# Wave attention: the value products of four heads in one call, two split heads of four, and the second half of every score on VectorE

## The chip, the cores and the metric

The kernel runs on one core of a Trainium2 chip. The metric is the device time of one execution in microseconds (us). The core has five engines with instruction streams of their own, in order and coupled by semaphores: TensorE (PE; its weight loads are listed as PEld), VectorE (DVE), ScalarE (ACT), GpSimd (POOL) and SyncE (SP), which here issues the DMAs.

## The reference, cut to what matters

Four blocks follow one another on x of 8 x 512 x 128: wave attention, a mixture of experts, an attention with distance terms, and the experts again, each on the layer-normed x and added to it. The change is in wave attention alone, which for 16 heads of 8 columns is:

```python
sim = jnp.einsum('bhid,bhjd->bhij', q, k) / sqrt(hd) / temp
scores = 0
for fi, freq in enumerate([31.0, 37.0, 41.0, 43.0, 47.0]):
    scores = scores + alpha[h, fi] * jnp.sin(TWO_PI * sim / freq + phi[h, fi])
w = sigmoid(scores); w = w / (w.sum(-1) + 1e-10)
out = jnp.einsum('bhij,bhjd->bhid', w, v)
```

So each of the 128 (batch, head) pairs has a 512 x 512 matrix, and each element of it takes five sines, five products with a head's factor, and a sigmoid.

## The kernel before

The heads are taken in NG = 32 groups of HG = 4; a head's 512 x 512 scores lie on 128 partitions as 2048 columns (four blocks kt of 512). Two groups are unrolled into `pair`, which a loop repeats. Head n = 4g + h passes through the engines as follows.

- **Scores.** TensorE makes them in two halves of 1024 columns (`make_scores`, L717, bf16) into psS, which holds one half at a time. Each half is copied to `s` as a fixed-point angle: the first half always by ScalarE (L792), the second by VectorE (L893) for heads in EVAC_HEADS and by ScalarE for the others. This runs two heads ahead of the sums.
- **Angles.** VectorE's `make_angles` turns `s` into the angles of frequencies 1, 2, 4 and 3, in that order (L880), and shifts frequency 4 (L917): five instructions, one head ahead. The angles of frequencies 1 to 3 are written into slots of the ring `score` (eight slots, one per head of two groups) that are free; for heads 2 and 3 some of these slots hold weights of the group before, and VectorE waits for `valued`. Before head 2 it is the last angle, frequency 3, that does. The angles of frequencies 0 to 3 are moved to `wave` by DMAs of 1 MB (L641, the queue SPq).
- **Sines.** ScalarE does five sines of 2048 columns in place (L827).
- **Sums.** TensorE adds frequencies 0 to 2 into psA (four PSUM banks, one copy) as products with diagonal matrices that GpSimd makes (L758). Frequencies 3 and 4 are added by VectorE in halves of 1024 columns (`add_sines`, L927). For a head in SPLIT_HEADS TensorE does frequency 2 for the first half alone, and VectorE adds the second half of it too, as its first instruction (`third`): five adds, without that four. The first add of frequency 3 for a half reads psA, the later ones read `score`. TensorE waits for `added` of the head before, half by half, before it writes psA again.
- **Weights.** ScalarE's `weigh` makes tanh(score / 2) in place (L802), for head n - 2 at the end of head n. The half that turns it into a sigmoid is applied with the column sums of V: L726 sums them into psV, `halve_values` (L923) halves them on VectorE after head 2.
- **Products with the values.** `values` (L734) multiplies the weights of group g - 1 with V, nine columns a head; head h takes rows 32h to 32h + 8 of psO, so a call of two heads goes to two column strips of the array, kt by kt, in turn. Heads 0 and 1 are done behind head 0 of group g, with the sums of L726 ahead of them, heads 2 and 3 behind head 2. `outputs` (L813) copies psO at the end of head 3, and a DMA stores it.

VectorE's order in head h is: angles of the next head, the copy of the second half of head h + 2's scores (if it is VectorE's), the adds of head h. TensorE's order in head h is: first scores of head h + 2, frequency 0, second scores, frequencies 1 and 2, then `values` for h = 0 and 2. The order is written out by hand. A credit (C_WEIGHED and the like) shifts each semaphore's count so that the first heads need no special case. Nothing else in the kernel is touched.

Of the kernel before, what the change touches and what calls it, by code (L numbers as in the profile page):

```python
# [18 lines left out]
H, HD = 16, 8  # L19
QT = L // P  # L20
NT = B * QT
HG = 4
NG = B * H // HG
GPB = H // HG
VW = HD + 1
# [8 lines left out]
MAX_POS = 256  # L34
FAR = 120.0
CARRIED = 4
SPLIT_HEADS = (0, 1, 2, 3)
EVAC_HEADS = (0, 2)
NEAR = 6.0


# [491 lines left out]
def wave_attention(nc, sb, ps, sem, a, V, ident, dram, params, bound):  # L533
# [13 lines left out]
    SR, AR = 2, 2 * HG  # L547
# [4 lines left out]
    CUTS = tuple(range(CARRIED, NF))  # L552
    NCUT = len(CUTS)
    C_SPS, C_SREADY, C_TURNED, C_CUT, C_SINE, C_USED, C_SUMMED = 2 * 2 * HG, 2, 2 * HG * (NF - 1), 2 * HG * NCUT, NF, 2 * PE_F, 4
    C_FIRST, C_VALUED, C_HALF, C_WEIGHED = 2, 4, 1, 2
    C_ADDED, C_DIAG, C_TAKEN, C_STORED = 2 * HG * ADDS, 2 * HG, 2, 16
    with ExitStack() as c:
        qp = sb(c, "qp", [NR, 2, HG, L], BF16)
# [16 lines left out]
        Vg = sb(c, "Vg", [P, 2, QT, HG, P // HG])  # L575
# [6 lines left out]
        psV = ps(c, "psV", [P, 1])  # L582
# [6 lines left out]
        valued = sem(c, "valued")  # L589
# [6 lines left out]
        v_ready = sem(c, "v_ready")  # L596
# [3 lines left out]
        weighed = sem(c, "weighed")  # L600
        out_taken = sem(c, "out_taken")
# [3 lines left out]
        v_summed = sem(c, "v_summed")  # L605
        half_ready = sem(c, "half_v_ready")
# [97 lines left out]
        @block.tensor  # L704
        def _(pe):
            for credit, n in ((s_ps, C_SPS), (s_ready, C_SREADY), (turned, C_TURNED), (first_ready, C_FIRST), (valued, C_VALUED), (cut, C_CUT), (sine, C_SINE),
                              (used, C_USED), (summed, C_SUMMED), (added, C_ADDED), (diag_ready, C_DIAG),
                              (out_taken, C_TAKEN), (half_ready, C_HALF),
                              (weighed, C_WEIGHED),
                              (out_stored, C_STORED)):  # L710
                pe.sem_inc(credit, n)

            def make_scores(n, u, h, half):
                pe.wait_ge(s_ready, n * 2 + half + C_SREADY)
                for k in range(2):
                    kt = half * 2 + k
                    mm = pe.matmul(psS[:, k, :], kp[:, u, h, kt * P:(kt + 1) * P], qp[:, u, h, :],  # L717
                                   start=True, stop=True)
                mm.then_inc(s_ps, 1)

            def values(g, slot, heads):
                if heads[0] == 0:
                    pe.wait_ge(v_ready, g + 1)
                    pe.wait_ge(half_ready, g + C_HALF)
                    for kt in range(QT):
                        mm = pe.matmul(psV[:], Vg[:, slot ^ 1, kt, :, :].rearrange("p h d -> p (h d)"),  # L726
                                       Vg[:, slot ^ 1, kt, 0, HD:VW], start=(kt == 0), stop=(kt == QT - 1))
                    mm.then_inc(v_summed, 1)
                    pe.wait_ge(out_taken, g + C_TAKEN)
                pe.wait_ge(weighed, g * HG + heads[-1] + 1)  # L730
                for kt in range(QT):
                    for h in heads:
                        row = h * (P // HG)
                        mm = pe.matmul(psO[row:row + VW, :],  # L734
                                       Vg[:, slot ^ 1, kt, h, 0:VW],
                                       score[:, slot * HG + h, kt * L:(kt + 1) * L],
                                       start=(kt == 0), stop=(kt == QT - 1), skip_group_check=True)
                mm.then_inc(valued, 1)

            def pair(gg, last):  # L740
                for u in range(2):
                    g = gg * 2 + u
                    for h in range(HG):
                        n = g * HG + h
                        more = not (last and u == 1 and h >= HG - 2)
                        nu, nh = (u, h + 2) if h < HG - 2 else (1 - u, h + 2 - HG)
                        if more:
                            if nh == 0:
                                pe.wait_ge(qk_loaded[nu], (gg + 1 + u) * 32)
                            make_scores(n + 2, nu, nh, 0)  # L750
                        pe.wait_ge(diag_ready, n + 1 + C_DIAG)
                        for f in range(PE_F):
                            pe.wait_ge(sine, n * NF + f + 1 + C_SINE)
                            for kt in range(2 if f == PE_F - 1 and h in SPLIT_HEADS else QT):
                                if f == 0 and kt % 2 == 0:

                                    pe.wait_ge(added, n * ADDS - ADDS + kt // 2 + 1 + C_ADDED)
                                mm = pe.matmul(psA[:, kt, :], diag[:, h % 2, f, :],  # L758
                                               wave[:, h % 2, f, kt * L:(kt + 1) * L],
                                               start=(f == 0), stop=(f == PE_F - 1 or (h in SPLIT_HEADS and f == PE_F - 2 and kt >= 2)),  # L760
                                               skip_group_check=True)
                                if f == PE_F - 1 and (kt % 2 == 1 or h in SPLIT_HEADS):
                                    mm.then_inc(summed, 1)
                            if f < PE_F - 1:
                                mm.then_inc(used, 1)
                            if more and f == 0:
                                make_scores(n + 2, nu, nh, 1)
                        if h in (0, 2):
                            values(g, 1 - u, (h, h + 1))

            pe.wait_ge(qk_loaded[0], 32)
            for h in range(2):
                for half in range(2):
                    make_scores(h, 0, h, half)
            with pe.Fori(0, NG // 2 - 1) as gg:
                pair(gg, False)
            pair(NG // 2 - 1, True)
            for h in (0, 2):
                values(NG, 1, (h, h + 1))

        @block.scalar
        def _(act):
# [13 lines left out]
            def weigh(m, at, general):  # L796
                act.wait_ge(added, (m + 1) * ADDS + C_ADDED)
                if general:
                    act.activation(score[:, at, :], score[:, at, :], ACT.Sigmoid).then_inc(weighed, 1)
                else:  # L800

                    act.activation(score[:, at, :], score[:, at, :], ACT.Tanh, scale=0.5).then_inc(weighed, 1)  # L802
# [13 lines left out]
            def pair(gg, last, general):  # L816
                for u in range(2):
                    g = gg * 2 + u
                    for h in range(HG):
                        n = g * HG + h  # L820
                        more = not (last and u == 1 and h >= HG - 2)
                        for f in range(NF):
                            if f < CARRIED:
                                act.wait_ge(carried[f][h % 2], (g * (HG // 2) + h // 2 + 1) * 16)
                            else:
                                act.wait_ge(cut, n * NCUT + CUTS.index(f) + 1 + C_CUT)
                            act.activation(wave[:, h % 2, f, :], angle[:, h % 2, f, :], ACT.Sin,  # L827
                                           scale=float(TWO_PI / 2.0 ** 32)).then_inc(sine, 1)
                            if f in (2, NF - 1) and more:
                                tu, th, tg = (u, h + 2, g) if h < HG - 2 else (1 - u, h + 2 - HG, g + 1)  # L830
                                if f == 2 or th not in EVAC_HEADS:
                                    take_scores(n + 2, tu, th, tg, f // 4, general)
                        weigh(n - 2, (u * HG + h - 2) % AR, general)
                        if h == HG - 1:
                            outputs(g, 1 - u, general)

            def all_heads(general):
                for h in range(2):
                    take_scores(h, 0, h, 0, 0, general)
                    if h not in EVAC_HEADS:  # L840
                        take_scores(h, 0, h, 0, 1, general)
                act.wait_ge(cleared, 2)
                with act.Fori(0, NG // 2 - 1) as gg:
                    pair(gg, False, general)
                pair(NG // 2 - 1, True, general)
                for h in (HG - 2, HG - 1):
                    weigh((NG - 1) * HG + h, HG + h, general)
                outputs(NG, 1, general)

            act.activation(og[:, 0:1], params[:, 0, 0, 0:1], ACT.Silu)  # L850
# [1276 lines left out]
```

## Time and profile before

| | |
|---|---|
| median of 3 runs (lowest to highest) | 3736.54 us (3734.22 to 3737.48) |
| the profiled execution: time, span | 3738.18 us, 3736.4 us |
| PE, DVE, ACT, POOL busy, share of the span | 84%, 81%, 71%, 26% |
| mean granted clock of TensorE | 0.937 of 2.4 GHz |
| the wave attention stage | about 105 to 1770 us of the span |

The span is that of the core's instructions. Busy shares count an engine as busy when an instruction of it runs; the wait before an instruction is shown with the one that released it. An f32 matmul of TensorE stands in the trace as two records, a bf16 one as one.

### The profile page before, as it was taken

The numbers are of one execution on the slowest core, as the hardware profiler recorded it, in microseconds if no ns is written. First come the engines' busy times: TensorE is split into PE (matmuls) and PEld (weight loads), VectorE is DVE, ScalarE is ACT, GpSimd is POOL, SyncE is SP. The second block draws the span as 40 slices with busy tenths as digits, with TensorE's granted clock in tenths as the row PEclk, the third lists the DMA queues.
The fourth block names the chain that finished last, engine by engine and source line by source line (L and its number), as shares of the span: only waits on it lengthen the run. The fifth ranks groups of instructions, "written<-read, shape, count | busy, mean of one in ns | idle before, by whom it ended". The sixth has DMA issues, their size and how long they took to land. (4 is left out here: it accounts for less than half of the span.)

```text
span 3736.4 us, 70767 instructions
## 1 busy us (share of the span) xinstructions
PE 3127.3 (84%) x26844; PEld 1990.0 (53%) x26844; DVE 3041.0 (81%) x4269; ACT 2656.2 (71%) x2265; POOL 981.3 (26%) x984
## 2 busy tenths in 40 slices
PE   3799999999999999998479715998998998998990
PEld 2233333333333333333358714888887887886890
DVE  8899999999999999997476545878878788786662
ACT  3899999999999999998134214776776776774430
POOL 2111111111111111110005344335245344330436
PEclk9899999999999999999679857999999999997995
DMA  5888899888999888996322227123113122112122
GB/s 163 300 332 343 335 340 346 334 337 337 345 342 340 333 343 337 341 342 253 115 74 60 55 75 183 24 32 51 28 28 51 28 36 42 28 19 74 44 61 68
DMA packets 311331, 683.36 MB, mean 183 GB/s; under 512 B 155296, under 2 KB 228608, under 8 KB 310560
## 3 DMA queue, kind: packets, MB, share of 16 engines
q1 hardware_dynamic: 302368, 661.87, 51.2%
q0 software_dynamic: 8704, 17.84, 2.0%
q8 instruction: 186, 3.05, 0.4%
q14 instruction: 73, 0.60, 0.1%
HBM read 90.73 MB, written 52.10 MB: 38 GB/s over the span
## 5 line engine op out<-in xcount | busy, mean ns | idle before, releaser
L758 PE MATMUL psA<-wave,diag 128*128 128x512 f32 x2560 | 1169.7, 604 | 81.5 <-DVE score L927 66.0
L827 ACT ACTIVATE wave<-wave 128x2048 f32<-128x2048 int32 x640 | 1186.8, 1908 | 44.8 <-DMA wave<-score 38.2
L758 PEld LDWEIGHTS psA<-wave,diag 128*128 128x128 f32 x2560 | 466.6, 190 | 687.7 <-issue 532.3
L880 DVE TENSOR_SCALAR score<-s,par 128x2048 int32<-128x2048 int32 x384 | 480.4, 1278 | 5.9 <-DMA wave<-score 5.8
L690 POOL TENSOR_TENSOR diag<-ident,par 128x128 f32<-128x128 f32 x384 | 143.0, 401 | 1268.7 <-PE psA L758 1268.2
L1850 POOL COPY kb<-ks 48x1024 bf16<-48x1024 bf16 x160 | 321.3, 2008 | 567.1 <-PE psR L1910 380.5
L927 DVE SCALAR_TENSOR_TENSOR score<-wave,par,score 128x1024 f32<-128x1024 f32 x384 | 469.6, 1277 | 0.0
L927 DVE SCALAR_TENSOR_TENSOR score<-wave,par,psA 128x1024 f32<-128x1024 f32 x256 | 315.6, 1274 | 46.7 <-PE psA L758 46.6
L2000 ACT ACTIVATE W<-psR 128x1024 f32<-128x1024 f32 x256 | 249.4, 1023 | 132.5 <-PE psR L1935 132.5
L1991 ACT COPY r<-psR 128x1024 f32<-128x1024 f32 x256 | 248.7, 1020 | 105.0 <-PE psR L1910 104.9
L2037 DVE TENSOR_REDUCE mx<-S 128x8 f32<-128x1024 f32 x256 | 305.4, 1214 | 2.2
L2030 DVE TENSOR_TENSOR S<-psR,S 128x1024 f32<-128x1024 f32 x192 | 234.5, 1221 | 57.0 <-PE psR L1926 56.7
L1935 PE MATMUL psR<-ident,S 128*128 128x128 f32 x2048 | 254.2, 277 | 27.9 <-DVE S L2045 27.9
L802 ACT ACTIVATE score<-score 128x2048 f32<-128x2048 f32 x130 | 247.9, 1907 | 3.5 <-DVE score L927 3.5
L1935 PEld LDWEIGHTS psR<-ident,S 128*128 128x128 f32 x2048 | 226.9, 142 | 40.2 <-DVE S L2030 11.8
L1991 ACT COPY S<-psR 128x1024 f32<-128x1024 f32 x192 | 185.6, 1022 | 82.9 <-PE psR L1910 82.9
L2045 DVE TENSOR_SCALAR S<-S,m 128x512 f32<-128x512 f32 x512 | 242.1, 541 | 0.6
L734 PE MATMUL psO<-score,Vg 128*9 128x512 f32 x1056 | 239.8, 596 | 3.0 <-ACT score L802 3.0
L792 ACT ACTIVATE s<-psS,par 128x1024 int32<-128x1024 f32 x192 | 212.1, 1105 | 11.6 <-PE psS L717 11.5
L1291 POOL DMA_INDIRECT f_xsS<-xn,f_token x144 | 139.5, 968 | 260.1 <-DVE f_token L1420 154.3
L1503 ACT ACTIVATE f_hT<-f_h 128x512 f32<-128x512 f32 x144 | 90.8, 631 | 163.3 <-DVE f_h L1457 163.2
L1926 PE MATMUL psR<-ident,r 128*128 128x128 f32 x1536 | 204.0, 277 | 0.0
(271 smaller groups left out, 4717.3 us busy)
## 6 DMA issues: line engine op xcount, KB each, us to landing
wave<-score SPq DMA_DIRECT2D x384, 1023.9 KB, 6.4
wave<-s SPq DMA_DIRECT2D x128, 1023.9 KB, 4.8
ks<-kb_parts SPq DMA_DIRECT2D x56, 384.0 KB, 6.1
qs<-qb_parts SPq DMA_DIRECT2D x32, 384.0 KB, 6.3
ys<-f_ys SPq DMA_DIRECT2D x36, 256.0 KB, 2.5
wave_out<-og SPq DMA_DIRECT2D x33, 256.0 KB, 7.2
o<-wave_out SPq DMA_DIRECT2D x8, 1024.0 KB, 5.3
qp<-qa_parts SPq DMA_DIRECT2D x32, 192.0 KB, 7.1
```

The lines of the kernel that those rows point to most:

```text
L734: mm = pe.matmul(psO[row:row + VW, :], Vg[:, slot ^ 1, kt, h, 0:VW], score[:, slot * HG + h, kt * L:(kt + 1) * L], start=(kt == 0), stop=( ...
L758: mm = pe.matmul(psA[:, kt, :], diag[:, h % 2, f, :], wave[:, h % 2, f, kt * L:(kt + 1) * L], start=(f == 0), stop=(f == PE_F - 1 or (h in ...
L802: act.activation(score[:, at, :], score[:, at, :], ACT.Tanh, scale=0.5).then_inc(weighed, 1)
L827: act.activation(wave[:, h % 2, f, :], angle[:, h % 2, f, :], ACT.Sin, scale=float(TWO_PI / 2.0 ** 32)).then_inc(sine, 1)
L880: dve.tensor_scalar(out, src, scalar, par[:, u, row, h * NF + f:h * NF + f + 1], ALU.mult, ALU.add).then_inc(done, 1)
L927: return dve.scalar_tensor_tensor(out=score[:, u * HG + h, cols], in0=wave[:, h % 2, f, cols], scalar=par[:, u, 1, h * NF + f:h * NF + f + ...
L1850: pool.tensor_copy(dst[rows, pairs, odd, :], src[rows, :, :].rearrange("r h (n two) -> r n h two", two=2)[:, pairs, :, odd]).then_inc(read ...
L1935: mm = pe.matmul(slot[:, i, kt * P:(kt + 1) * P], S[:, 2 * j + i, kt * P:(kt + 1) * P], ident[:], start=(kt == 0), stop=True, is_transpose ...
L1991: act.copy(dst[:, :, k * CP:(k + 1) * CP], psR[:, n % RING, :, :].rearrange("p a (n h) -> p h (a n)", h=BH)).then_inc(act_took, 1)
L2000: act.activation(W[:, pair % RING_W, :, :].rearrange("p a n -> p (a n)"), psR[:, n % RING, :, :].rearrange("p a n -> p (a n)"), ACT.Exp, s ...
L2037: dve.tensor_reduce(mx[:, hs, kt], S[:, hs, kt * P:(kt + 1) * P], AX.X, ALU.max).then_inc(maxed, 1)
L2045: dve.tensor_scalar(S[:, h, :], S[:, h, :], m[:, h:h + 1], None, ALU.subtract).then_inc(shifted, 1)
```

## The change

SPLIT_HEADS becomes (0, 2): for heads 1 and 3 TensorE sums frequency 2 whole, and VectorE has four adds. EVAC_HEADS becomes (0, 1, 2, 3): VectorE copies the second half of every head's scores. `values` handles all four heads in one call, kt by kt with the four strips in turn, and stands in head 1 between frequency 0 (with the second scores) and frequency 1; it waits for the weights of all four heads of the group before, and `valued` rises by 2 at once. `weigh` handles head n - 1, so that these weights are there in time, and its credit rises to 3.

```diff
-SPLIT_HEADS = (0, 1, 2, 3)
-EVAC_HEADS = (0, 2)
+SPLIT_HEADS = (0, 2)
+EVAC_HEADS = (0, 1, 2, 3)
...
-    C_FIRST, C_VALUED, C_HALF, C_WEIGHED = 2, 4, 1, 2
+    C_FIRST, C_VALUED, C_HALF, C_WEIGHED = 2, 4, 1, 3
...
-            def values(g, slot, heads):
-                if heads[0] == 0:
-                    pe.wait_ge(v_ready, g + 1)
-                    pe.wait_ge(half_ready, g + C_HALF)
-                    for kt in range(QT):
-                        mm = pe.matmul(psV[:], Vg[:, slot ^ 1, kt, :, :].rearrange("p h d -> p (h d)"),
-                                       Vg[:, slot ^ 1, kt, 0, HD:VW], start=(kt == 0), stop=(kt == QT - 1))
-                    mm.then_inc(v_summed, 1)
-                    pe.wait_ge(out_taken, g + C_TAKEN)
-                pe.wait_ge(weighed, g * HG + heads[-1] + 1)
+            def values(g, slot):
+                pe.wait_ge(v_ready, g + 1)
+                pe.wait_ge(half_ready, g + C_HALF)
                 for kt in range(QT):
-                    for h in heads:
+                    mm = pe.matmul(psV[:], Vg[:, slot ^ 1, kt, :, :].rearrange("p h d -> p (h d)"),
+                                   Vg[:, slot ^ 1, kt, 0, HD:VW], start=(kt == 0), stop=(kt == QT - 1))
+                mm.then_inc(v_summed, 1)
+                pe.wait_ge(out_taken, g + C_TAKEN)
+                pe.wait_ge(weighed, g * HG + HG)
+                for kt in range(QT):
+                    for h in range(HG):
                         row = h * (P // HG)
                         mm = pe.matmul(psO[row:row + VW, :],
                                        Vg[:, slot ^ 1, kt, h, 0:VW],
                                        score[:, slot * HG + h, kt * L:(kt + 1) * L],
                                        start=(kt == 0), stop=(kt == QT - 1), skip_group_check=True)
-                mm.then_inc(valued, 1)
+                mm.then_inc(valued, 2)
...
                             if more and f == 0:
                                 make_scores(n + 2, nu, nh, 1)
-                        if h in (0, 2):
-                            values(g, 1 - u, (h, h + 1))
+                            if f == 0 and h == 1:
+                                values(g, 1 - u)
...
-            for h in (0, 2):
-                values(NG, 1, (h, h + 1))
+            values(NG, 1)
...
-                        weigh(n - 2, (u * HG + h - 2) % AR, general)
+                        weigh(n - 1, (u * HG + h - 1) % AR, general)
...
-                for h in (HG - 2, HG - 1):
-                    weigh((NG - 1) * HG + h, HG + h, general)
+                weigh(NG * HG - 1, AR - 1, general)
```

## Rows read from the trace of the kernel before

**Rows 1.** Busy time of each engine in the wave stage; columns in its first line

```profile
core 0: us, PE busy (x) PEld busy (x) DVE busy (x) ACT busy (x) POOL busy (x), PEclk, DMA share, GB/s
...
170.00:1680.00 1510.00, 1420.44 (x4003) 525.43 (x4002) 1472.89 (x1263) 1469.91 (x910) 221.53 (x410) 1.00 0.90 339
```

**Rows 2.** Waits of VectorE and ScalarE, 170 to 1680 us: total, times, longest

```profile
DVE score L927 <- PE psA L758: 37.0, 45, 1.5
...
ACT wave L827 <- DMA wave<-score: 33.3, 65, 1.2
```

**Rows 3.** The halving of the value sums: first of 33, and group 19

```profile
L923 DVE TENSOR_SCALAR half_v<-psV x33: 144/148/153, 159.1 to 1763.5; 128x1 f32<-128x1 f32 x33
...
1136.50 0.15 DVE L923 TENSOR_SCALAR half_v<-psV 128x1 f32<-128x1 f32 x1
```

**Rows 4.** Time line of VectorE, head 0 into head 1: start, us, operation

```profile
1000.54 1.27 DVE L893 TENSOR_SCALAR s<-psS,par 128x1024 int32<-128x1024 f32 x1
1001.74 2.46 DVE L927 SCALAR_TENSOR_TENSOR score<-wave,par,psA 128x1024 f32<-128x1024 f32 x2
1004.12 3.67 DVE L927 SCALAR_TENSOR_TENSOR score<-wave,par,score 128x1024 f32<-128x1024 f32 x3
...
1012.49 1.21 DVE L917 TENSOR_SCALAR wave<-wave 128x2048 int32<-128x2048 int32 x1
1014.61 2.47 DVE L927 SCALAR_TENSOR_TENSOR score<-wave,par,psA 128x1024 f32<-128x1024 f32 x2 [0.91 <-PE psA L758]
```

**Rows 5.** Time line of TensorE's matmuls, heads 0 to 2 of the same group

```profile
1000.90 0.95 PE L726 MATMUL psV<-Vg 128*128 128x1 f32 x8
1001.78 3.61 PE L734 MATMUL psO<-score,Vg 128*9 128x512 f32 x16
1005.32 0.60 PE L717 MATMUL psS<-qp,kp 48*128 48x512 bf16 x2
...
1010.02 5.42 PE L758 MATMUL psA<-wave,diag 128*128 128x512 f32 x12
1015.37 0.60 PE L717 MATMUL psS<-qp,kp 48*128 48x512 bf16 x2
1017.14 3.70 PE L758 MATMUL psA<-wave,diag 128*128 128x512 f32 x8 [1.17 <-DVE score L927]
1020.77 0.60 PE L717 MATMUL psS<-qp,kp 48*128 48x512 bf16 x2
1021.30 5.42 PE L758 MATMUL psA<-wave,diag 128*128 128x512 f32 x12
```

**Rows 6.** Time line of ScalarE: the copy of the first scores in head 1

```profile
1006.38 1.10 ACT L792 ACTIVATE s<-psS,par 128x1024 int32<-128x1024 f32 x1
```

**Rows 7.** TensorE's groups in the second attention, 2340 to 3400 us

```profile
L1935 PE MATMUL psR<-ident,S 128*128 128x128 f32 x2048 | 254.2, 277 | 27.9 <-DVE S L2045 27.9
...
L1951 PE MATMUL psDO<-W,Vb 128*9 128x128 f32 x4096 | 135.8, 273 | 0.0
```

**Rows 8.** Time lines of TensorE behind idle time (in brackets); two windows as in rows 1

```profile
399.56 5.39 PE L758 MATMUL psA<-wave,diag 128*128 128x512 f32 x8 [1.73 <-ACT wave L827]
...
862.62 3.70 PE L758 MATMUL psA<-wave,diag 128*128 128x512 f32 x8 [1.65 <-ACT wave L827]
...
1765.61 5.30 PE L734 MATMUL psO<-score,Vg 128*9 128x512 f32 x16 [2.98 <-ACT score L802]
...
2309.06 1.04 PE L1910 MATMUL psR<-kb,T 112*128 112x64 bf16 x16 [3.40 <-POOL kb L1850]
...
2312.25 0.63 PE L1910 MATMUL psR<-kb,T 112*128 112x64 bf16 x16
...
2322.07 0.89 PE L1923 MATMUL psR<-ks,qs 112*128 112x128 bf16 x8 [2.00 <-ACT W L1991]
...
3363.88 1.94 PE L1935 MATMUL psR<-ident,S 128*128 128x128 f32 x16 [2.21 <-DVE S L2045]
...
3367.45 1.91 PE L1935 MATMUL psR<-ident,S 128*128 128x128 f32 x16
...
400.50:404.50 4.00, 4.00 (x7) 1.54 (x5) 4.00 (x4) 4.00 (x4) 0.00 (x0) 0.57 0.69 262
...
2322.50:2326.00 3.50, 3.50 (x38) 3.44 (x36) 1.22 (x1) 0.44 (x1) 3.01 (x2) 0.55 0.00 0
```

## The prediction

> **What bounds the kernel now.** I read the slices of the page first: the stage of wave attention fills the first half of the span, and the rest is untouched by the change. Over 1,510 us of that stage VectorE is busy for 1,472.9, ScalarE for 1,469.9, TensorE for 1,420.4, at a granted clock of 1.00 (2.4 GHz) [rows 1]. With three engines so full, busy shares decide nothing, so the waits came next: VectorE waits 37.0 us in the stage, and only for TensorE's sums in psA; ScalarE waits 33.3 us for angles carried by DMA [rows 2]. Then the period: the halving of the value sums starts at 159.1 for group 0 and at 1136.50 for group 19, so a group takes 977.4 / 19 = 51.44 us [rows 3]. The 37.0 us are 1.26 per group (1,510 / 51.44 = 29.4 groups); VectorE's own work is the other 50.18. VectorE is in order and nearly full, so the period changes by what its instructions and its waits change.
>
> The time lines show where its waits arise. psA has one copy. TensorE may start head n's first frequency only when VectorE's first add of frequency 3 (the first `added` of head n-1) has read it, and VectorE may start head n's adds only when TensorE has summed again. I call that add's start s. VectorE's pace is 1.19 us an instruction [rows 4]. In [rows 4] the two-instruction row at 1014.61 holds the split add and that add, so s = 1015.80; TensorE starts at 1017.14, s + 1.34 [rows 5]. Its pieces, start to start [rows 5]: frequency 0, 3.63 us (1017.14 to 1020.77); a pair of score matmuls 0.53 (to 1021.30); frequency 1 and half of frequency 2, 5.35 (1010.02 to 1015.37); the sums of values 0.88 and the products of two heads 3.54 (1000.90, 1001.78, 1005.32). Now those 3.54 stand right behind heads 0 and 2, where TensorE would otherwise wait for VectorE's add.
>
> **The change part by part.**
>
> *Split heads (0, 2).* Two VectorE adds go: -2 x 1.19 = -2.38 us a group. TensorE gets two more f32 products in heads 1 and 3 each: a product is 3.44 / 4 = 0.86 (16 records of a 128x512 product at two records each; eight last 3.63 with their tail), so +3.44 a group.
>
> *Second halves of all scores on VectorE.* +2 x 1.20 = +2.40 us a group there, which cancels the above; ScalarE loses two copies of some 1.10 each [rows 6], -2.2 a group. ScalarE's relief is worth its waits at most, and it is not what VectorE waits for. I cost it at nothing.
>
> *`weigh` one head earlier.* The same four per group. It waits for the adds of head n-1; these end 4 x 1.19 = 4.8 us after s, and ScalarE still has the sines of the next head to do. Nothing.
>
> *Four heads at once.* The eight calls for a pair occupy 16 records in 3.54 us; two heads share the array. The new order interleaves four column strips. The nearest row is the second attention, which already does it with 128 columns: 4,096 records in 135.8 us, 33 ns each, where full-width records take 254.2 / 2048 = 124 ns [rows 7]. That is 3.7 to one, so all four heads should take 3.54 once, saving 3.54 per group, against the +3.44. The other bound is pairs only: 7.08. I take 3.54.
>
> *Its new place.* This is the term that matters. The call now stands inside head 1, between frequency 0 and frequency 1, so it is on the path from the first add of head 0 to the first add of head 1, and the idle time behind heads 0 and 2 that covered it is given up. From s of head 0, TensorE needs 1.34 + 3.63 + 0.53 + 0.88 + 3.54, then frequency 1 and, unsplit, kt 0 and 1 of frequency 2: 12 records, 5.42 with their tail, and 0.03 until VectorE starts: s + 15.37. VectorE has that add and three more, five instructions of angles and a copy, ten in all: s + 11.95. It waits 3.42 us. (Within this time `valued` also holds the fourth angle; that wait lies inside the same 3.42, because the sums come last. Queued behind it are the cut and the copy, and the DMA of angle 3 of head 2 starts about 1.7 us later, with over 5 us before its sine is needed.) The second add needs kt 2 and 3, another 1.72, where VectorE is ready after 1.19: +0.53. Together **3.95 us per group, in head 1**.
>
> Head 3, also unsplit: TensorE is ready at s + 1.34 + 3.63 + 0.53 + 5.45 = s + 10.95, VectorE at s + 12.0, and the second add leaves 0.5. No wait, slack 0.5. Heads 0 and 2: TensorE needs 10 records and no values, 1.34 + 3.63 + 0.53 + 4.6 = 10.1 after the add before, VectorE comes at 11.9 or later. The scores' second half in head 1 waits for ScalarE's copy, which in [rows 6] ends at 1007.48, or s + 4.55 with s = 1002.93; TensorE asks at s + 4.97. Nothing.
>
> *The clock.* TensorE now idles before the odd heads. Head 0 with the score pair behind it ends 3.63 + 0.53 + 5.35 + 0.53 = 10.04 us after its start, at (s of head 3) + 11.4; the next start is (s of head 3) + 11 x 1.19 + 1.34 = + 14.4: a gap of 3.0 us. Before head 3, counted from head 1's late sums, 2.6. Today's regular gap is 1.17 [rows 5]. What larger gaps do is in [rows 8]: after 1.73 idle at 399.56 eight records took 5.39 instead of 3.70, at a granted clock of 0.57 over 4 us; after 2.98 sixteen took 5.30 instead of 3.61 (1765.61); after 3.40 and 2.00 the next stretches were also slow (granted 0.55 near 2322.5); after 1.65 and after 2.21 nothing. So of four gaps between 2.0 and 3.4, three were followed by 1.2 GHz, and each costs TensorE about 1.65 us. In head 1 there is no slack: 0.75 x 1.65 = +1.24. In head 3, 0.5 of slack: 0.75 x 1.1 = +0.83.
>
> The Trainium skill, "TensorE: Matmul & The Clock Gate", section "HAM oscillation — how this bites in real kernels", makes only waits longer than either of these gaps drop the clock; by it the sum would be 3824. Here the trace disagrees: 1.73 us sufficed once.
>
> *Sum.* (3.95 + 1.24) x 32 = +166.1; 0.83 x 31 = +25.7; the waits of now go, -1.26 x 32 = -40.3. At the end of the stage the products of all heads wait for the last `weigh`, behind a gap of 2.98 + 3.61 = 6.6 us instead of 2.98: bounds 0 and 1.7, by the row at 1765.61 nearer +1. In all +152.5. The profiled execution took 3738.2 us (span 3736.4, 1.8 around it), so **3890.7 us, say 3890**; the runs' median, 3736.5, lies 1.6 below it.
>
> **Rivals.**
>
> *A. The same wait, but the clock stays.* Idle gaps of 1.65 and 2.21 us kept it [rows 8]. Then 3.95 x 32 - 40.3 = +86: **3824**. If instead it falls at every gap: (3.95 + 1.65) x 32 + 1.1 x 31 - 40.3 = +173: 3911, the upper end of the forecast's own range, 3850 to 3920. Chance of A 0.17, of the forecast 0.70.
>
> *B. Four strips do not run at once with 512 columns.* Pairs only: 7.08 us for the products, +3.54 x 32 = +113 on the forecast: **4004**. Against it stand the 33 ns of [rows 7]. Chance 0.05. The same page, "Measured speedup vs the span model", gives 2.38 times for three strips; by a factor near that the products would last about 1.4 us longer per group than my term, an estimate from that page, and the time 3935.
>
> *C. Faster: the wait in head 1 does not arise.* If TensorE's path from the add of head 0 to the sums of head 1 fitted into VectorE's 11.95 us, only VectorE's 50.18 per group would remain: 3738.2 - 40.3 = **3698**, with ScalarE's 2.2 us of relief keeping it out of the way. It decides below 11.95; I count 15.37, and even with the products free it would be 11.83 plus the 0.5 of the second add. Chance 0.04.
>
> The rest, 0.04, is for mixtures, among them no net change.
>
> **How the numbers follow.** Rival A's 3824 and the forecast's top of 3911 hold 0.87; the range is 3812 to 3925, leaving out B, C and the tails. Within 0.2% (7.5 us) a measurement of this kernel cannot tell a change. Faster 0.04 (C), same 0.02, slower 0.94.
>
> **What would show it.** After: a group of about 56.3 us (54.1 under A); VectorE waiting some 5 us per group on psA, nearly all at head 1's first two adds, and part of it at the fourth angle on `valued`; idle TensorE gaps of 2.6 to 3.0 us before frequency 0 of heads 1 and 3; granted clock near 0.95 in the stage; 32 records of products in about 3.6 us; ScalarE's busy time down by 2.2 a group and its idle up. The prediction is wrong if the products last 7 us (B), if the clock stays at 1.00 (A), or if VectorE's wait at head 1 is under 3 us.

## The result and the profile after

The changed kernel takes 3886.4 us (median of 4 runs, 3882.3 to 3892.1) against 3735.4 for the kernel before: a ratio of 1.0408, 95% interval 1.039 to 1.0426. It is slower by 151 us; 3890 was forecast. The profiled execution took 3892.1 us, its span 3890.3.

Busy time by engine in the wave stage and VectorE's waits there, of the changed kernel; these lines answer to [rows 1, 2]:

```profile
170.00:1650.00 1480.00, 1341.50 (x3790) 516.01 (x3788) 1333.69 (x1138) 1288.42 (x767) 152.94 (x371) 0.96 0.83 312
...
DVE score L924 <- PE psA L757: 82.8, 106, 1.7
DVE score L877 <- PE psO L733: 63.5, 26, 3.4
...
PE psA L757 <- DVE score L924: 94.0, 53, 1.8
PE psS L717 <- DVE s L890: 44.4, 53, 0.8
```

The halving of the value sums, whose starts gave the period in [rows 3], first and in group 17 (954.2 us later):

```profile
L920 DVE TENSOR_SCALAR half_v<-psV x33: 140/145/152, 164.0 to 1915.6; 128x1 f32<-128x1 f32 x33
...
1118.21 0.14 DVE L920 TENSOR_SCALAR half_v<-psV 128x1 f32<-128x1 f32 x1
```

A group takes 954.2 / 17 = 56.13 us instead of 51.44. That is 4.69 more, and 32 times it is 150, so the groups alone carry the loss. In a stretch of 1,480 us (26.4 groups) VectorE waits 146.3 us, 5.55 a group, where it was 1.26. There is a second kind of wait now, at an angle (L877) for the products with the values (psO). TensorE's granted clock is 0.96 instead of 1.00. VectorE has as many instructions a group as before. The three engines that were nearly full are all less busy: for VectorE, which sets the period, the loss is waiting, not work.

Time lines of VectorE and then TensorE, from head 0's adds to head 1's, in a group where the clock stayed (compare [rows 4, 5]):

```profile
1026.00 2.46 DVE L924 SCALAR_TENSOR_TENSOR score<-wave,par,psA 128x1024 f32<-128x1024 f32 x2
...
1037.45 1.29 DVE L877 TENSOR_SCALAR score<-s,par 128x2048 int32<-128x2048 int32 x1 [1.81 <-PE psO L733]
...
1042.76 1.28 DVE L924 SCALAR_TENSOR_TENSOR score<-wave,par,psA 128x1024 f32<-128x1024 f32 x1 [1.70 <-PE psA L757]
1044.48 1.28 DVE L924 SCALAR_TENSOR_TENSOR score<-wave,par,psA 128x1024 f32<-128x1024 f32 x1 [0.44 <-PE psA L757]
```

```profile
1026.14 0.60 PE L717 MATMUL psS<-qp,kp 48*128 48x512 bf16 x2 [0.83 <-DVE s L890]
1028.52 3.70 PE L757 MATMUL psA<-wave,diag 128*128 128x512 f32 x8 [1.77 <-DVE score L924]
1032.24 0.60 PE L717 MATMUL psS<-qp,kp 48*128 48x512 bf16 x2
1032.77 1.05 PE L725 MATMUL psV<-Vg 128*128 128x1 f32 x8
1033.76 3.62 PE L733 MATMUL psO<-score,Vg 128*9 128x512 f32 x32
1037.31 7.13 PE L757 MATMUL psA<-wave,diag 128*128 128x512 f32 x16
```

The three waits of VectorE add up to 1.81 + 1.70 + 0.44 = 3.95 us, the number forecast for head 1. The products of four heads take 32 records in 3.62 us. And here is what was forecast otherwise: TensorE's idle time in front of head 1 is not one gap of 3.0 us but 0.83 and 1.77, with a pair of score matmuls between them that waits for VectorE's copy (L890).

The next group, where the clock fell; TensorE, then VectorE:

```profile
1083.96 5.40 PE L757 MATMUL psA<-wave,diag 128*128 128x512 f32 x8 [1.77 <-DVE score L924]
1089.29 0.60 PE L717 MATMUL psS<-qp,kp 48*128 48x512 bf16 x2
```

```profile
1094.50 1.29 DVE L877 TENSOR_SCALAR score<-s,par 128x2048 int32<-128x2048 int32 x1 [3.41 <-PE psO L733]
...
1099.81 1.28 DVE L924 SCALAR_TENSOR_TENSOR score<-wave,par,psA 128x1024 f32<-128x1024 f32 x1 [1.70 <-PE psA L757]
```

The same gap of 1.77 us, but the eight records of frequency 0 take 5.40 instead of 3.70, and VectorE's first wait grows from 1.81 to 3.41, by all but 0.1 of it. Of 54 such gaps in front of heads 1 and 3 between 170 and 1700 us, 15 were followed by eight records in 3.70 and 39 by 5.2 to 5.4: 0.72 of them, where 0.75 was forecast from other gaps. The two heads are not alike, though: the clock fell behind all 27 gaps in front of head 3, and behind 12 of the 27 in front of head 1.

### The profile page after: what moved, and what is told of

Its sections match the earlier page's. It is cut to its first block and busy times, and to the rows that moved or that the text cites. A ratio compares the mean times of both kernels' runs of the same rounds, so it can differ in the third digit from the quotient of the medians.

```text
span 3890.3 us, 71150 instructions
## 1 busy us (share of the span) xinstructions
PE 3213.7 (83%) x27100; PEld 2050.8 (53%) x27100; DVE 3050.8 (78%) x4269; ACT 2610.9 (67%) x2200; POOL 927.3 (24%) x984
## 5 line engine op out<-in xcount | busy, mean ns | idle before, releaser
L757 PE MATMUL psA<-wave,diag 128*128 128x512 f32 x2816 | 1356.7, 633 | 115.0 <-DVE score L924 115.0
L825 ACT ACTIVATE wave<-wave 128x2048 f32<-128x2048 int32 x640 | 1199.0, 1904 | 147.5 <-DMA wave<-score 127.2
L757 PEld LDWEIGHTS psA<-wave,diag 128*128 128x128 f32 x2816 | 543.3, 200 | 844.0 <-issue 671.3
L877 DVE TENSOR_SCALAR score<-s,par 128x2048 int32<-128x2048 int32 x384 | 480.3, 1278 | 84.0 <-PE psO L733 79.0
L924 DVE SCALAR_TENSOR_TENSOR score<-wave,par,score 128x1024 f32<-128x1024 f32 x320 | 393.2, 1276 | 0.0
L717 PE MATMUL psS<-qp,kp 48*128 48x512 bf16 x512 | 156.4, 386 | 79.1 <-DVE s L890 59.1
L790 ACT ACTIVATE s<-psS,par 128x1024 int32<-128x1024 f32 x128 | 140.9, 1101 | 98.7 <-PE psS L717 98.7
```

The source lines that it names most:

```text
L757: mm = pe.matmul(psA[:, kt, :], diag[:, h % 2, f, :], wave[:, h % 2, f, kt * L:(kt + 1) * L], start=(f == 0), stop=(f == PE_F - 1 or (h in ...
L877: dve.tensor_scalar(out, src, scalar, par[:, u, row, h * NF + f:h * NF + f + 1], ALU.mult, ALU.add).then_inc(done, 1)
L924: return dve.scalar_tensor_tensor(out=score[:, u * HG + h, cols], in0=wave[:, h % 2, f, cols], scalar=par[:, u, 1, h * NF + f:h * NF + f + ...
```

## The experiments

Ten kernels were run. Each was compared with runs of the kernel before on the same chip (3739.6 to 3740.2 us there, where it took 3735.4 beside the changed kernel). So differences from the changed kernel are given by times and, where it matters, by ratios, which are the safer numbers.

**1. The two tuples of heads alone.**

```diff
-SPLIT_HEADS = (0, 1, 2, 3)
-EVAC_HEADS = (0, 2)
+SPLIT_HEADS = (0, 2)
+EVAC_HEADS = (0, 1, 2, 3)
```

> The kernel before with the two tuples of heads alone changed (split heads 0 and 2, copies of all heads on VectorE); the products stay in two calls behind heads 0 and 2. My theory: VectorE's 42 instructions a group stay 42, TensorE gets 3.4 us more, and heads 1 and 3 have 1.1 to 1.2 us of waits together, as many as before: 3735 within 15. Rival (the added TensorE work sets the period, or ScalarE's relief pays): 3790 or more, or 3700.

3737.8 us, ratio 0.9991 (0.9981 to 1.0001): no difference. Its waits in 1,480 us:

```profile
DVE score L927 <- PE psA L758: 35.1, 87, 0.6
```

About as much as the 37.0 in [rows 2], in 1,510 us, but spread over 87 short waits. TensorE's 3.4 us more a group found room, and ScalarE's relief bought nothing.

**2. The call for four heads and the earlier `weigh` alone.** The changed kernel with both tuples as before.

```diff
-SPLIT_HEADS = (0, 2)
-EVAC_HEADS = (0, 1, 2, 3)
+SPLIT_HEADS = (0, 1, 2, 3)
+EVAC_HEADS = (0, 2)
```

> The changed kernel with the two tuples of heads as before: four split heads, copies of heads 0 and 2 on VectorE. So only the call for four heads, its place, and the earlier weigh are new. My theory: TensorE comes 0.9 us sooner with head 1's sums, VectorE 1.2 sooner, so the wait there is about 3.75 and the clock costs as much again as in the changed kernel: about 3875. Rival (the loss needs the unsplit heads): 3780 or less.

3894.7 us, ratio 1.0412 (1.0391 to 1.0433), the changed kernel's own loss. So the loss is in this part. The size was 20 us over my number. TensorE has 106 waits for VectorE's adds in 1,480 us, where the changed kernel has 53, but the 53 added are in front of heads 0 and 2, 48 of them of 1.17 or 1.18 us, and no slow records followed any of them. What differs is head 1: slow records followed 20 of 27 gaps there (7 of them took 6.6 us), where in the changed kernel it was 12 of 27. VectorE's waits for psO are 85.5 us, where the changed kernel has 63.5.

**3. The call moved behind head 0.**

```diff
-                            if f == 0 and h == 1:
-                                values(g, 1 - u)
+                        if h == 0:
+                            values(g, 1 - u)
```

> The changed kernel, with the call for four heads moved from inside head 1 to behind head 0 (sums of V and products, 4.4 us). My theory (the call is on TensorE's path between two adds of VectorE, and the idle time behind head 0 that used to cover it is lost): TensorE starts head 1 at s + 2.7 instead of s + 1.34 but needs 4.4 us less inside it, so VectorE waits 0.4 + 0.5 us there instead of 3.95 and more; the gap in front of head 3 and its low clock stay (0.8). A group of about 52, a time of about 3755. Rival (the products of four strips are dear wherever they stand, or the new split of the adds is): about as slow as the changed kernel, 3880.

3769.1 us, ratio 1.0070 (1.0053 to 1.0087). Moving a call of the same instructions by one frequency gives back 3.4 of the 4.1 points; the time is 14 us above the 3755 expected. VectorE waits 57.7 us in 1,480 for psA and no longer for psO: some 26 of them in front of head 1's sums, which is the 0.9 a group expected there, and 32 in front of head 3's, where the gap stays, 1.1 a group instead of 0.8.

**4. The products as two pairs, one behind the other, in head 1.**

```diff
+                for first_head in (0, 2):
                     for kt in range(QT):
-                    for h in range(HG):
+                        for h in (first_head, first_head + 1):
```

> The changed kernel with the products in head 1 as two calls of two heads one behind the other, so that they last 7.1 us instead of 3.6. My theory (this stretch lies on the critical path without slack): all of the 3.5 us shows, 32 times, +113: 4000, and VectorE's wait at the fourth angle of head 2 grows by 3.5. Rival (the loss is VectorE's or the DMAs' and TensorE's stretch is partly covered): under 3950.

3973.9 us (2 runs), ratio 1.0625. Over the changed kernel that is 0.0217 x 3738, some 81 us or 2.5 a group, less than the 113 expected. The time line of TensorE has the reason:

```profile
1016.99 5.34 PE L734 MATMUL psO<-score,Vg 128*9 128x512 f32 x32
```

The products took 5.34 us and not 7.1, 1.7 more than in the changed kernel, so the doubling that I meant to make was not made. The other 0.8 goes together with a clock that is lower still (0.94 in the stage; in front of this row eight records took 6.58). That lengthening the stretch in head 1 lengthens the group is shown; that it does so one for one is not shown by this run alone.

**5. TensorE kept busy in the gaps.** Six small products of no use in front of heads 1 and 3, into spare columns of the bank of the value sums; the halving moves behind head 1.

```diff
...
+                        if h in (1, 3):
+                            pe.wait_ge(half_ready, g + h // 3 + C_HALF)
+                            for _ in range(6):
+                                pe.matmul(psV[:, P:2 * P], ident[:], ident[:], start=True, stop=True,
+                                          skip_group_check=True)
                         pe.wait_ge(diag_ready, n + 1 + C_DIAG)
```

> The changed kernel plus six small f32 products (128 columns, some 1.4 us) of no use on TensorE in front of heads 1 and 3, into spare columns of the bank of the value sums; VectorE's halving of the sums moves from behind head 2 to behind head 1, so that this bank is free. It computes the same result. My theory (a part of the loss is TensorE's lower clock behind the idle gaps): the granted clock stays at 1.00, VectorE waits only 3.95 a group, 3824. Rival (the clock is off the path, or its fall is not a matter of these gaps): 3885.

3871.3 us, ratio 1.0346 (1.0329 to 1.0363). The clock no longer fell behind the gaps (0.99 in the stage), yet only 15 us came back (23 by the ratios), nearer to the rival. Its waits of VectorE and TensorE, and TensorE's time line in head 1:

```profile
DVE score L882 <- PE psO L733: 83.6, 27, 4.6
DVE score L929 <- PE psA L762: 57.8, 54, 1.7
...
PE psS L717 <- ACT s L795: 23.8, 27, 1.5
...
1017.51 3.70 PE L762 MATMUL psA<-wave,diag 128*128 128x512 f32 x8 [0.24 <-DVE score L929]
1021.87 0.60 PE L717 MATMUL psS<-qp,kp 48*128 48x512 bf16 x2 [0.66 <-ACT s L795]
```

VectorE still waits 141.4 us, because a new wait stands in the path: once frequency 0 is no longer slow, TensorE asks for the second scores before ScalarE has copied the first. ScalarE's sine ahead of that copy waits for a DMA:

```profile
1018.90 1.91 ACT L830 ACTIVATE wave<-wave 128x2048 f32<-128x2048 int32 x1 [0.58 <-DMA wave<-score]
1020.72 1.10 ACT L795 ACTIVATE s<-psS,par 128x1024 int32<-128x1024 f32 x1
```

The wait is 0.9 us a group. In 7 of 27 groups the clock also fell behind it, and the products took up to 5.32 us instead of 3.62:

```profile
299.58 0.60 PE L717 MATMUL psS<-qp,kp 48*128 48x512 bf16 x2 [1.04 <-ACT s L795]
300.11 1.05 PE L725 MATMUL psV<-Vg 128*128 128x1 f32 x8
301.09 5.32 PE L733 MATMUL psO<-score,Vg 128*9 128x512 f32 x32
```

That is 7 / 27 x 1.7 = 0.4 a group more. The 3.95 of head 1 with these 0.9 and 0.4 is 5.3 us a group, which is what VectorE waits (141.4 us in 26.7 groups). To see whether the wait for ScalarE hides the clock's cost, the next two runs exchange the call and the second scores, with and without the small products.

**6. The call ahead of the second scores, clock kept.**

```diff
+                            if f == 0 and h == 1:
+                                values(g, 1 - u)
                             if more and f == 0:
                                 make_scores(n + 2, nu, nh, 1)
-                            if f == 0 and h == 1:
-                                values(g, 1 - u)
```

> The kernel with small products in front of heads 1 and 3, which still took 3871, with one exchange inside head 1: the call for four heads ahead of the second scores instead of behind them. In that kernel TensorE waits some 0.9 us a group at the second scores for ScalarE's copy of the first, whose sine waits for a DMA. My theory (this wait is why keeping the clock gave 15 us and not 62): ahead of it stand 4.4 us of products now, so it goes, VectorE's waits come down to 3.95 a group, 3826 to 3835. Rival (the wait for ScalarE is only a symptom): 3870.

3821.6 us, ratio 1.0219 (1.0204 to 1.0235), where the prediction's rival A, the same wait with the clock kept, had 3824. No wait for ScalarE at the scores is left, no product call was slow, and VectorE's two waits are 72.2 and 27.5 us in 1,480, 3.6 a group:

```profile
DVE score L929 <- PE psA L762: 72.2, 54, 2.2
DVE score L882 <- PE psO L733: 27.5, 28, 1.0
```

**7. The same exchange without the small products.**

> The changed kernel with the call for four heads ahead of the second scores in head 1, and no small products. In the changed kernel TensorE does not wait for ScalarE at the second scores (its slower clock gives ScalarE the time). My theory: nothing changes, 3886 within 6; the exchange only pays where the clock is kept (3822 with both, 3871 with the small products alone). Rival (the exchange shortens the path by itself): 3840 or less.

3918.2 us, ratio 1.0496 (1.046 to 1.0532). Both views were wrong: it is some 30 us slower than the changed kernel. The granted clock is 0.93 in the stage, and the rows behind the gaps show a third length:

```profile
1028.10 6.57 PE L757 MATMUL psA<-wave,diag 128*128 128x512 f32 x8 [1.77 <-DVE score L924]
...
1059.87 5.40 PE L757 MATMUL psA<-wave,diag 128*128 128x512 f32 x8 [1.77 <-DVE score L924]
...
1086.13 6.57 PE L757 MATMUL psA<-wave,diag 128*128 128x512 f32 x8 [1.78 <-DVE score L924]
```

From about 890 us on the group repeats every 58.03 us with the same pattern; before that it takes 55.2 to 56.9. Of 52 gaps 8 were followed by 3.70 us, 31 by 5.3 to 5.4 and 13 by 6.57 or 6.58, all 13 in front of head 1; in the changed kernel none was that long. So gaps of one length, 1.77, are followed by three different costs. The granted clock (the third number from the end) around 1028.10 and 1059.87 shows what differs:

```profile
1026.00:1028.00 2.00, 0.32 (x2) 0.00 (x0) 2.00 (x3) 1.85 (x1) 0.08 (x1) 0.77 1.01 418
1028.00:1030.00 2.00, 1.90 (x3) 0.87 (x4) 2.00 (x3) 1.41 (x2) 0.00 (x0) 0.50 0.79 328
...
1057.00:1059.80 2.80, 0.60 (x2) 0.11 (x2) 2.80 (x4) 1.73 (x2) 0.85 (x3) 1.00 1.01 418
1059.80:1062.00 2.20, 2.13 (x4) 1.01 (x5) 2.20 (x3) 2.20 (x2) 0.00 (x0) 0.82 0.29 119
1062.00:1064.00 2.00, 2.00 (x4) 0.82 (x3) 2.00 (x4) 2.00 (x2) 0.00 (x0) 0.50 0.85 315
```

Ahead of the 6.57 the clock had fallen within the gap (0.77 there, then 0.50, which is 1.2 GHz). Ahead of the 5.40 it was still 1.00 through the gap and fell only once the records ran. What sets the moment, and why this order meets the dear one so often, is open. With the exchange in, keeping the clock is worth 97 us (3918 to 3822; 104 by the ratios); without it 15 (23).

**8. A place for each part.** The changed kernel with the products behind head 0 and the sums of V behind head 2.

```diff
-                            if f == 0 and h == 1:
-                                values(g, 1 - u)
+                        if h == 0:
+                            values(g, 1 - u)
+                        if h == 2:
+                            value_sums(g, 1 - u)
```

> The changed kernel with the products of four heads behind head 0 and the sums of V behind head 2, each in idle time of TensorE. My theory: head 1's sums come at s + 11.5 where VectorE needs 11.95, so no wait there; in front of head 3 the gap stays long enough for the clock to fall in most groups, 0.7 a group; a group of 50.9, 3720. Rival (TensorE's added work of unsplit heads, or ScalarE and the DMAs behind it, keep the period): 3735 or more.

3752.6 us, ratio 1.0034 (1.0021 to 1.0048), not 3720. VectorE's waits are 39.7 us in 1,480, as many as before the change. Some 29 of them are in front of head 3's sums, where 1.0 a group stands against the 0.7 expected, and eight records took up to 6.73; the other 10 are in front of head 1's, where none was expected:

```profile
1033.06 6.73 PE L760 MATMUL psA<-wave,diag 128*128 128x512 f32 x8 [1.78 <-DVE score L930]
```

**9 and 10. A version faster than both, and what the clock is worth in it.** The products stay behind head 0, the sums of V go inside head 2, behind its first frequency, and are halved ahead of its adds; six small products stand in front of head 3. Then the same without them.

```diff
-                            if f == 0 and h == 1:
-                                values(g, 1 - u)
+                            if f == 0 and h == 2:
+                                value_sums(g, 1 - u)
                         if h == 0:
                             values(g, 1 - u)
...
+                        if h == 3:
+                            pe.wait_ge(half_ready, g + 1 + C_HALF)
+                            for _ in range(6):
+                                pe.matmul(psV[:, P:2 * P], ident[:], ident[:], start=True, stop=True,
+                                          skip_group_check=True)
```

> As the kernel with products behind head 0, but the sums of V inside head 2 (behind its first frequency), their halving on VectorE ahead of head 2's adds, and six small products of no use in front of head 3 to keep TensorE's clock. It computes the same result. My theory: the clock stays at 1.00, VectorE waits 0.1 to 0.4 a group, 50.4: 3705. Rival (the fall of the clock there costs nothing, or the DMAs bound the loop): no better than the kernel without the small products.

3719.5 us, ratio 0.9945 (0.9931 to 0.9958): 20 us faster than the kernel before, by less than forecast. The clock is 1.00 and little waiting is left:

```profile
170.00:1650.00 1480.00, 1457.92 (x4566) 585.34 (x4568) 1466.84 (x1259) 1412.51 (x848) 312.34 (x413) 1.00 0.91 344
...
DVE score L935 <- PE psA L765: 12.5, 34, 0.4
```

> The kernel with products behind head 0, sums of V inside head 2 and small products in front of head 3, but without those small products. My theory: the gap in front of head 3 is again some 1.8 us behind a wait for VectorE's copy, the clock falls behind it in most groups, VectorE waits 0.7 to 1.1 a group more than with the small products: 3742 to 3755, against 3719 with them. Rival (the place of the sums of V made the gain, not the clock): 3720.

3731.0 us, ratio 0.9979 (0.9969 to 0.9988), 28.2 us of VectorE's waits in 1,480 and a clock of 0.98. This lies between the two views. So the small products are worth 11 us here (13 by the ratios), and the better place of the sums of V and of their halving about 21 (from 1.0034): the rival was half right.

## Why the prediction was right

**What bounds the kernel.** VectorE's instructions and its waits for TensorE set the period. It held: its own work is 50.18 us a group before and (1,480 - 146.3) / 26.4 = 50.6 after. The 0.4 more was not forecast. It is in part the 0.08 by which neighbouring instructions overlap, which is lost at each of some five waits a group (before, 1.5).

**The tuples of heads** were costed at nothing: the run with them alone is at 0.9991.

**The products** were taken at 3.54 us for all four heads; 3.62 from first start to last end, 3.55 to the next start. Rival B fell with that row, and so did the 1.4 us more that is set beside it as an estimate, for which the prediction shows no working.

**The new place.** Forecast 3.95 us a group in head 1, measured 3.95 where the clock stays: 3.51 and 0.44 for the forecast 3.42 and 0.53, so two small errors cancel in the last digit. The run with the call behind head 0 confirms the term. So does the one with the clock kept and the exchange (3822 against 3824), though its wait is 3.6 and not 3.95.

**The clock.** Forecast: three gaps of four, +1.24 in head 1 and +0.83 in head 3, 5.19 + 0.80 = 6.0 us of waits in all; measured 0.72 of the gaps and 5.55 us. Within the changed kernel's own trace its price is plain, 3.41 against 1.81 in the same wait. But the share of three quarters was read from four gaps of other lengths behind other work, and it agrees only as a mean. With 12 of 27 gaps followed by the lower clock in front of head 1, VectorE's waits there are 4.5 a group instead of 5.19; with 27 of 27 in front of head 3, they are 1.0 instead of 0.80. That the groups' part of the sum came out (4.69 x 32 = 150 against 151.5) is in part luck: the waits are 0.44 a group less than forecast, VectorE's own work 0.4 more.

Three more parts of the reasoning were off without moving the sum much. The gaps are 1.77 us behind a wait of 0.83, not 3.0 and 2.6: I left out that TensorE's first scores wait for VectorE's copy of the head before. ScalarE's busy time fell from 50.1 to 48.9 us a group, by 1.2 and not by 2.2. And the price of the clock cannot be read as what would come back if the clock were kept, as rival A's 3824 does: without the exchange only 15 us did. What failed there is the "nothing" for ScalarE's copy in head 1, whose slack I had as 4.97 - 4.55 = 0.4 us. In the run with the clock kept the copy is 0.9 late on average. In the changed kernel it costs nothing, but only just. In the group shown above, where the clock stayed in head 1, the copy

```profile
1031.09 1.10 ACT L790 ACTIVATE s<-psS,par 128x1024 int32<-128x1024 f32 x1
```

ends at 1032.19, and the second scores start at 1032.24. Whether the slow records in front of head 3, there in every group, are what keeps it in time is not shown.

**The page's rule on longer waits**, cited in the prediction from the Trainium skill, "TensorE: Matmul & The Clock Gate", section "HAM oscillation — how this bites in real kernels", would have kept the clock at the 2.6 to 3.0 us forecast. It does not hold here: gaps of 1.77 us, behind a wait of 0.83 and 0.60 of score matmuls, were followed by the lower clock 39 times of 54.

**Rival C**, that the wait would not arise, has its measure in the kernel with products behind head 0 and kept clock: 3719.5, not 3698. It needs another place for the call.

## What to carry to other kernels

Cost an edit by where it stands on the path between two engines that hand one buffer back and forth, not by its busy time: the same 4.4 us of matmuls cost most of 4% inside head 1 and, with all other edits kept, less than 1% behind head 0, one frequency earlier. When work is taken out of an engine's idle time, look at what that idle time does to its clock and to the next waits. And price a cure by a run, not by the wait it removes, because a second wait just behind may take its place (only 15 us of the 62 forecast came back until the order was changed too).

## What the runs showed of the hardware

A gap of one length in front of the same instructions was followed by three durations of eight f32 records of 512 columns: 3.70, 5.40 and 6.57 us. Where they took 5.40 the granted clock was 1.00 through the gap and fell behind it, where they took 6.57 it had fallen within the gap. It fell at shorter waits too: in 7 of 27 groups of the run with the small products it was behind a wait of 0.7 to 1.2 us. What sets the moment was not settled.

Two calls of 16 records on different column strips, one behind the other, took 5.34 us together where one takes 3.61. The weight loads of that call come two to a row at most times, and four to six in the middle:

```profile
1018.28 0.10 PEld L734 LDWEIGHTS psO<-score,Vg 128*9 128x9 f32 x2 [0.33 <-issue]
1018.71 0.12 PEld L734 LDWEIGHTS psO<-score,Vg 128*9 128x9 f32 x6 [0.33 <-issue]
1019.14 0.12 PEld L734 LDWEIGHTS psO<-score,Vg 128*9 128x9 f32 x4 [0.31 <-issue]
```

I read this as the second pair starting while the first was still running. Shown is that an order by pairs costs less than twice one pair.
